# Self attention of four layers: queries and keys turned once per entry in a compact layout and unfolded through DRAM, row maxima brought in by transfer, and a layer's first entry prepared before the last feed-forward entry

## The reference

```
for l in range(4):
    h = rmsnorm(x, n1[l])
    q, k, v = split(h @ Wqkv[l].T + bqkv[l])          # 16 heads of 8 features
    q, k = apply_rope(q, cos, sin), apply_rope(k, cos, sin)
    x = x + merge_heads(softmax(q k^T / sqrt(8) + causal_bias) v) @ Wo[l].T + bo[l]
    ... cross attention on the context, masked by seg_ids, added to x
    x = x + silu(h3 @ Wg[l].T) * (h3 @ Wu[l].T) @ Wd[l].T
```

## Time and profile before

| what | value |
|---|---|
| three runs | 2101.96, 2107.96, 2116.95 us (median 2107.96) |
| span of the profiled execution, first to last instruction | 2100.9 us |
| mean granted TensorE clock, 1 is 2.4 GHz | 0.940 |
| busy share: PE, DVE, ACT, POOL | 87%, 67%, 51%, 37% |
| first score tile of layers 0 and 1 | 646.48 us, 1025.64 us |

### The profile page before, as it was taken

The page is one execution under the profiler, slowest core; times in us unless marked ns, Lnnn a source line. Parts: engine busy times, 40 slices in busy tenths (PEclk is TensorE's granted clock), DMA queues, the critical chain, the costliest instruction groups (busy, mean ns, idle before and its releaser), DMA issues. The chain is left out here.

```text
span 2100.9 us, 34690 instructions
## 1 busy us (share of the span) xinstructions
PE 1827.5 (87%) x13011; PEld 1120.1 (53%) x13011; DVE 1415.5 (67%) x3427; ACT 1067.7 (51%) x1523; POOL 784.6 (37%) x1131
## 2 busy tenths in 40 slices
PE   5978998594777898899999999999999989989978
PEld 4557664373544444564544565644555554456557
DVE  8667776543676877864577885567786467787475
ACT  2655655131453566564466566366656446656510
POOL 4423324403624453431455342245443155443130
PEclk9999999597787898998999999999999999999989
DMA  7443333121000000141000033000014000003200
GB/s 227 111 137 101 109 104 97 63 69 39 21 1 13 1 1 13 37 110 43 16 1 1 1 93 84 28 1 1 1 44 120 14 16 2 1 26 99 52 1 21
DMA packets 69995, 100.91 MB, mean 48 GB/s; under 512 B 17126, under 2 KB 35438, under 8 KB 69188
## 3 DMA queue, kind: packets, MB, share of 16 engines
q1 hardware_dynamic: 60612, 90.01, 14.9%
q0 software_dynamic: 9216, 8.69, 1.6%
HBM read 52.43 MB, written 12.38 MB: 31 GB/s over the span
## 5 line engine op out<-in xcount | busy, mean ns | idle before, releaser
L1806 DVE TENSOR_REDUCE maxima<-wide 128x2 f32<-128x512 f32 (+3 forms) x512 | 406.1, 819 | 134.2 <-PE wide L836 130.7
L2042 ACT ACTIVATE prob<-wide 128x768 f32<-128x768 f32 (+1 forms) x384 | 332.2, 881 | 149.7 <-PE wide L836 149.4
L1965 ACT ACTIVATE prob<-wide 77x1024 f32<-77x1024 f32 x256 | 257.8, 1017 | 89.8 <-PE wide L836 86.5
L836 PE MATMUL wide<-q_g 32*128 32x256 f32 (+3 forms) x2048 | 268.5, 394 | 37.5 <-ACT prob L2042 18.1
L2284 POOL TENSOR_SCALAR_AFFINE_SELECT prob<-prob 128x256 f32<-128x256 f32 (+1 forms) x384 | 184.9, 487 | 296.4 <-ACT prob L2042 294.6
L1482 DVE TENSOR_REDUCE maxima<-wide 128x8 f32<-128x616 f32 x256 | 202.9, 795 | 110.7 <-PE wide L836 106.7
L836 PEld LDWEIGHTS wide<-q_g 32*128 32x128 f32 x2048 | 140.0, 188 | 205.6 <-issue 100.1
L2106 POOL TENSOR_TENSOR rstd<-moments,cst 128x4 f32<-128x4 f32 x88 | 90.4, 1027 | 360.7 <-DVE moments L1370 173.8
L1886 ACT ACTIVATE q_g<-wide 128x1024 fp32r<-128x1024 f32 x128 | 131.1, 1024 | 179.3 <-PE wide L836 177.4
L1886 ACT ACTIVATE q_g<-acc 128x512 fp32r<-128x512 f32 x192 | 114.5, 596 | 144.0 <-PE acc L836 139.0
L2191 POOL DMA_DIRECT2D masked_k<-kx x224 | 121.2, 546 | 177.4 <-PE wide L836 176.3
(11 more groups left out here) (253 smaller groups left out, 3096.1 us busy)
## 6 DMA issues: line engine op xcount, KB each, us to landing
masked_q<-q_g SPq DMA_DIRECT2D x448, 64.0 KB
masked_q<-mask_l SPq DMA_DIRECT2D x84, 308.0 KB
masked_k<-kx POOLq DMA_DIRECT2D x224, 19.5 KB, 1.9
A<-in_w SPq DMA_DIRECT2D x2, 2048.0 KB, 12.2
unit_w<-in_unit_w SPq DMA_DIRECT2D x8, 448.0 KB, 3.9
ffn_w<-in_ffn_w SPq DMA_DIRECT2D x4, 768.0 KB, 4.7
slots_in<-v_third SPq DMA_DIRECT2D x1, 2560.0 KB, 12.6
prob<-slots_in SPq DMA_DIRECT2D x8, 320.0 KB, 3.1
```

The lines of the kernel that those rows point to most:

```text
L836: return e.matmul(out, lhsT, rhs, start=start, stop=stop, is_transpose=turn)
L1806: e.tensor_reduce(top[:, t, h], v[:, :, at0:at0 + P * t + P], AX.X, ALU.max, negate=True).then_inc(*made("max", *([("free", tile)] if t == ...
L1965: e.activation(p[0:SC, :], s[0:SC, :], ACT.Exp, bias=0.0, scale=1.0).then_inc(*made("exp", pb, ("free", tile)))
L2042: e.activation(pv, sv, ACT.Exp, bias=0.0, scale=8 ** -0.5).then_inc(*made("exp", pb, ("free", tile)))
```

## The change

Each kept as in the two files, cut to its core.

1. `qk_turn` is done once per entry instead of once per group. The rotated queries and keys are turned as they are, without the padding: 8 turns for an entry, and ACT copies the [128 x 1024] tile into the front of `qkv` (`raw_qk`). The weights' columns are reordered on the host (`by_feature`) so that the 32 rows of a group lie together.
2. `qk_cut` then cuts in the turned layout: DVE one high part of 1024 columns, POOL one difference of 1024 columns. `cut_q`, `cut_k` and `k_tok` go.
3. `qk_store` writes the parts to a DRAM scratch tensor `qk_rows` (one of three) with three DMAs of 512 KB on SP's queue, in the row layout that the matmuls want. `qk_fetch` brings one group's [128 x 1024], 512 KB, back into `q_g`, one DMA for each group. The rows for the ones are put in the scratch at the start of the program.
4. `self_full` turns only the maxima, one turn of [128 x 32]. ACT copies 32 x 128 numbers to `mx_t`, and the new step `self_max` is a DMA on SP's queue that writes them in 8 rows of `q_g`.
5. The rows at which the steps stand are other ones, and `begin` and `turned` of layer l+1 are an item of their own between the third and the fourth `f3` entry.
6. The tables for the rotation are four times as wide and are loaded into `cst` during the program; POOL clears less of `A`.

```diff
     def prepare(b, g):
         if (l, b, g) == (0, 0, 0):
-            return in_rows((11, ("qk_turn", l, b, g)))
+            return in_rows((13, ("qk_fetch", l, b, g)))
+        phase, c = in_rows((4, ("qk_fetch", l, b, g))), b + 1
...
-        phase, c = in_rows((8, ("qk_turn", l, b, g))), b + 1
-        if b and g == 0:
-            phase = beside(in_rows((2, ("cut_k", l, b))), phase)
         if c < B:
             phase = beside(phase, *[[normalise(c)],
                                     [project_in(c), rotate(c, (0, 10))],
-                                    [rotate(c, (1, 1), (2, 3), (3, 6), (4, 8))],
-                                    [rotate(c, (5, 1)), in_rows((4, ("cut_q", l, c)))]][g])
+                                    [rotate(c, (1, 1), (2, 3), (3, 6), (4, 8), (5, 11))],
+                                    [spread(c, 1, 4, 9)]][g])
...
+    def spread(b, *rows):
+        return in_rows(*zip(rows, (("qk_turn", l, b), ("qk_cut", l, b), ("qk_store", l, b))))
...
     def attend(b, g):
-        return in_rows((1, ("self_full", l, b, g)), (4, logits(0, 2)), (6, logits(0, 0)), (8, logits(1, 2)),
-                       (10, logits(1, 0)), (12, ("self_values", l, b, g, 0)))
+        return in_rows((1, ("self_full", l, b, g)), (2, ("self_max", l, b, g)), (8, logits(0, 2)), (10, logits(0, 0)))
...
-    turned = beside(rotate(0, *[(k, k // 2) for k in range(6)]), in_rows((3, ("cut_q", l, 0)), (3, ("cut_k", l, 0))),
+    turned = beside(rotate(0, *[(k, k // 2) for k in range(6)]), spread(0, 3, 3, 4),
...
-            every[-1] = [beside(every[-1][0], project)] + every[-1][1:]
-            every.append(rotate)
+            every.insert(len(every) - 1, [project] + rotate)
...
+            def qk_store(l, b):
+                for w in need(("sq_top", l, b), ("sq_cut", l, b), T.freed("qk_rows", held)):
+                    e.wait_ge(*w)
+                e.dma_start(to[:, 0, :], t[:, 1:3, :]).then_inc(*landed(f"store_qk{at}"))
+                e.dma_start(to[:, 1, :], t[:, 1::2, :]).then_inc(*landed(f"store_qk{at}"))
+                e.dma_start(to[:, 2, :], t[:, 0::2, :]).then_inc(
+                    *landed(f"store_qk{at}", ("qk_stored", l, b), ("free", ("sqt", l, b))))
+
+            def qk_fetch(l, b, g):
+                for w in need(("qk_stored", l, b), ("qk_rows",), T.freed("q_g", held)):
+                    e.wait_ge(*w)
+                e.dma_start(q_g[at][:, :, :].rearrange("p k s -> p (k s)").bitcast(F32), of[:, 2 * S * g:2 * S * g + 2 * S]).then_inc(
+                    *landed(f"fetch_qk{at}", ("sqk_copied", l, b, g), ("free", ("qk_rows", l, b))))
+
+            def self_max(l, b, g):
+                for w in need(("mx_turned", l, b, g)):
+                    e.wait_ge(*w)
+                e.dma_start(qk[SELF_MAX:P:SELF_STEP, 0, :].bitcast(F32), mx_t[at].bitcast(F32)).then_inc(
+                    *landed(f"store_max{at}", ("sq_filled", l, b, g), ("free", held)))
...
-            def qk_turn(l, b, g):
+            def qk_turn(l, b):
...
-                for w in need(("sq_cut", l, b), ("sk_cut", l, b)):
-                    e.wait_ge(*w)
-                turn_queries(s[:, 0:S], cut_queries(("sqt", l, b)), g)
-                turn_queries(s[:, S:2 * S], k_tok, g).then_inc(*made("q_turn", tile))
+                for w in need(("rotated", l, b)):
+                    e.wait_ge(*w)
+                for k in range(2):
+                    for t in range(NI):
+                        i_mm = mm(s[:, S * k + P * t:S * k + P * t + P], src[:, t, k, :], ident, turn=True)
+                i_mm.then_inc(*made("q_turn", tile))
...
-                turn_queries(a, cut_queries(("sqt", l, b)), g).then_inc(
-                    *made("q_turn", tile, *([("free", ("sqt", l, b))] if g == G - 1 else [])))
+                mm(a[0:2 * HG * NI, 0:P], maxima_in[g % 2][:, :, :, :].rearrange("p i k t -> p (i k t)"), ident,
+                   turn=True).then_inc(*made("q_turn", tile))
```

206 lines of the change are left out of this document (115 added, 91 removed).

## The result

The changed kernel takes 2219.39 us (median of 4 runs, 2209.89 to 2230.1) against 2105.51 us for the kernel before in the same comparison. The ratio is 1.0541, interval 1.0495 to 1.0587: 5.4% slower, outside the forecast range (2056 to 2136). The profiled execution has a span of 2210.3 us, 109.4 more than before.

The account below looks back on a forecast made before the run. PE was taken to bound the steady self attention. The terms -64 + 12 + 7 + 22 + 10 = -13 us, from 2107.96, gave 2095 us; range 2056 to 2136, the forecast's own 2076 to 2114, chance 0.42.

Parts of the forecast that it names:

- The saving: Self attention groups: fewer turns relieve PE of 1.17 us a group; 64 us taken as saved, between 38 and 75.
- The entries: At 12 entries inside layers, PE waits about 1 us each for POOL's rotation: 12 us lost, 0 to 30.
- The path's durations: DRAM path: store 6 us, bounds 5 and 9; fetch 3.8 us, between 3.3 and 4.4.
- Start of layer 0: From rotation of entry 0 to first score tile, the new chain through store and fetch loses 7 us, 0 to 14.
- Starts of layers 1 to 3: First score tile 7.5 us later at each start, through rotation, turns, store and fetch: 22 us, 9 to 39.
- Filling and draining: At each layer's start 1.5 us and end 1 us lost around the maxima: 10 us over four layers, 0 to 15.
- rival 2: Layer starts also lose the clock, 5 us at each of four: +24 us, 2132 us, chance 0.20.
- Rival 1: DRAM path covered: POOL never late inside layers, a start costs 3 us: -50 us, 2058 us, chance 0.28.
- rival 4: Maxima come too late in every group, needing more than 5 us from self_full to logits; given no case.
- Rival 3: DVE takes over: a group can't go below 10.4 us, saving 38 us, sum +13, 2121 us; chance 0.10.

Follow-up runs that it names:

- before_no_turns: Kernel before with one of each four self-attention turns kept, its columns copied four times, nothing in place of the others: 2100.08 us, ratio 1.0014.
- before_new_rows: Kernel before with only the changed kernel's new rows of attend and finish, turns and copies as before, no DRAM path: 2130.37 us, ratio 1.0162.
- after_real_turns: Changed kernel with spare fp32 identity turns, eight ahead of each group's first score tile and three at self_full: 2213.75 us, ratio 1.0567.
- no_turns_new_rows: Kernel before with one of each four self-attention turns kept and the new rows of attend and finish, no DRAM path: 2117.26 us, ratio 1.0141.
- the old join: Changed kernel with the next layer's first entry prepared beside the last f3 entry again, as in the kernel before: 2191.47 us, ratio 1.0466.
- after_two_turns: Changed kernel with two spare fp32 identity turns ahead of each group's first score tile: 2186.93 us, ratio 1.0386.

## Why the prediction was wrong, point by point

**The saving.** The price of the turns held. With the clock's deficit taken out, the score stretches need at most 700 - 621 = 79 us less. I had 64, less 12 for the entries and 10 for filling and draining, so 42: the saving was at its upper end, and two of the losses were small. The sign that I had named, 10.1 us for a steady group of layer 1, reads so in the changed kernel:

```profile
L1859 DVE TENSOR_TENSOR maxima_in<-maxima,maxima_in x11: 174/175/1118, 1102.0 to 1220.8; 128x16 f32<-128x16 f32 x11
```

Ten groups take 118.8 us, 11.9 each, longer than the 11.1 of before. The granted clock of that stretch is 0.87; 118.8 x 0.87 / 10 = 10.3 us would be left at the higher level. So the forecast's arithmetic held for a clock of 1.00, and only for that. before_no_turns tells what such a saving is worth by itself: 75 us of turns gone, nothing gained.

**The entries.** 12 us forecast, 7.0 measured behind the rotation. Store and fetch inside a layer were covered: PE waited for no fetch there.

**The path's durations.** Store 6 against 5.84 us, fetch 3.8 against 3.99, all by rows of other transfers. The estimate by the Trainium skill, DMA: Bandwidth & Descriptors, Anatomy of one DMA, was 5.6 and 3.2 us; both are a little short of what this trace shows. That section gives its figures for DMAs issued from GpSimd, and these are issued from SP.

**Start of layer 0.** Forecast 7 us, measured 15.27 - 8.23 = 7.0.

**Starts of layers 1 to 3.** Forecast 7.5 each, measured 10.0 each (28.25 - 18.26), 30 in all instead of 22, inside its bounds of 9 to 39. The chain was right, its size was off by 2.5 us. Layer 1 has them in three pieces: the rotation took 7.93 us (1031.98 to 1039.91) instead of 7.44; the eight turns took 1.94 us instead of 0.97, as they ran at the lower level (0.50 from 1040 to 1043 us); and PE came to the score tile 1.0 us after the fetch had landed, at 1057.12 against 1052.12 + 4.0. What I had forecast as the last wait, that for the fetch, was therefore none in layers 1 to 3. The wait behind the rotation was 2.86 us, not 4 to 6, since PE had stood 5.17 us for DVE's normalising of the last `f3` entry just before. I had not seen that wait coming; it took nothing from the chain, as PE stood again right behind it.

**Filling and draining.** Forecast 10 us. PE waits 14.6 us for the cut maxima of the self attention and 5.4 for those of the cross attention, which have a line of their own now; before it was 13.8 for both together. That is 6 us more. The new rows alone bring 9 (before_new_rows, 23.2 us), so it is they more than the transfer that cost here.

**The step that failed** is in rival 2, as the prediction put it: "If 10 us of PE's work then run at the lower level, 5 us are lost at each of the four starts." And the sum behind it took for granted that the steady groups keep the clock of 1.00 of the earlier trace rows. The starts lost 90 - 30 = 60 us of clock, 15 each; inside the layers, where I had put nothing, the deficit rose by 127 - 15 = 112 us. Rival 2 had the right sign and the right resource, at an eighth of the size: its clock term was 20 us, the deficit grew by 168. The prediction counted the turns only as time that PE spends, and not as work that holds its clock. In the forecast itself the term that failed is the -64: in before_no_turns, taking nine of twelve turns away is worth +3 us instead, and in after_real_turns putting eleven back costs nothing. And the new rows, part of the change, had no term at all; alone they cost 34 us. The earlier trace rows showed what the turns cost; nothing in the profile of before showed a group without them.

**The other rivals.** Rival 1 had it right that the path through DRAM is covered inside the layers, and rival 4 was rightly given no case: PE waited for one fetch and for no transfer of maxima. Rival 3 asked for DVE above 85% busy; in the score stretch of layer 1 it is busy 128.93 of 188.8 us, 68%.

**The cause, as far as the runs carry it.** *Shown:* full-width PE work in the groups brings the granted clock back. Taken out of the kernel before, it costs 45 us of deficit (60 by the middle of the executions); put back in the changed kernel, it returns 108, with PE standing still as long as without it; two turns a group return 54 inside, eleven in the first entries 40 at the starts (these two from one profile each). *Shown:* for the time this makes the turns worth about nothing, in either kernel. So their loss explains why nothing was saved, and not the whole 5.4%. *Shown:* the rows cost 34 us, 21 of deficit. *Likely:* the new join costs some 16 us, nearly all as time and not as clock.

By the ratios, turns and rows together make 30 us (no_turns_new_rows), and the changed kernel stands 114 above before. The 84 us between are less well divided. Two spare turns in every group take 33 of them away, the old join 16, and the forecast's own terms, 7 us at the start of layer 0 and 7 us of waits at the twelve entries, account for 14. These were not tried together, and the last 20 us or so stay open.

*Open:* why the starts lose more clock in the changed kernel and in after_two_turns (90 and 92 us) than in no_turns_new_rows (54), whether the transfers add up to 30 us of deficit, and what it is about a 128x128 turn that the groups' own matmuls (32x128 and 128x32 weights) lack. All spare work here was full-width. No run put in as much narrow work, so more PE work of any shape might do the same.

The Trainium skill, TensorE: Matmul & The Clock Gate, HAM oscillation, lays a lost clock to waits between bursts of matmuls. For the fall this trace agrees in part: the clock fell within the wait of 2.17 us at 1065 to 1067 us. For what follows it differs: the clock stayed at 0.50 for 36 us in which PE was busy for 35.58. The measurement decides, so waits are not enough as a rule here. That the low stretch at a layer's first groups lasts some 37 us instead of 10 makes about 3 x 27 / 2 = 40 of the 168 us.

In the forecast's own terms: -79 for the score stretches at the full clock, +141 of deficit in them, and +47 outside them, 26 of them deficit, make the 109 measured. The four starts, forecast at 7 + 22 us and measured at 7 + 30, lie in these 47 us, with their own share of the deficit.

## What to carry to other kernels

Before taking work off PE, ask what share of its full-width work that is, and read the granted clock as a resource of the stretch beside its busy time: a kernel at 1.00 may be there because of the work that looks redundant. When the change is built, compare span times (1 - clock) before and after, stretch by stretch and over several executions, ahead of any chain of waits. A cheap probe helps: put spare full-width matmuls back, and if they cost no time, the clock was paying for them. The probe finds the cause and need not give the time back: eleven turns a group gained nothing here, three bf16 matmuls or two turns 33 to 36 us of the 114.

## What the runs showed of the hardware that I had not expected

- The lower level can hold for 36 us while PE has work all the time: 0.50 from 1067 to 1103 us, with 35.58 us busy. It began within a wait of 2.17 us. With eleven more full-width turns a group, the low stretch at the same place lasted 10 us. A matmul into `wide` from `q_g` took 458 ns on the mean, against 394 before.
- Eleven more fp32 turns in each of 64 groups took no time (1.0567 against 1.0541), and 75 us of turns less gained none (1.0014).
- For a load of 436 KB over 109 partitions SP waited up to 19.3 us; one of 384 KB over 96 partitions landed in 3.3 us. The Trainium skill, DMA: Bandwidth & Descriptors, Why a DMA increments its semaphore by 16 and not by 1, says that the number of engines is the largest up to 16 that divides the slowest dimension, so one engine for a prime count; the two durations agree with that.
- Four DVE normalisings of 128x128 took 3.86 us while POOL rotated, against 0.366 us each on the mean; what held them up was not tried.
